# Filler products and a bias product 64 columns wide, fewer fillers, and no mark of each pair's buffer, in a fused attention and feed-forward kernel

## What is computed

```python
xn = layernorm(x)                                   # without weights
# attention: 16 heads of 64
a = layernorm(xn) * ln_w + ln_b
q, k, v = (einsum('bsd,hde->bshe', a, W) + b for W, b in ((W_q, b_q), (W_k, b_k), (W_v, b_v)))
p = softmax(causal(q k^T * 64 ** -0.5))
attn = einsum('bqhe,hed->bqd', p v, W_o) + b_o
# feed-forward, weights rounded to -1, 0, 1 by their mean magnitude
ffn = relu(xn Wq1^T + b1) Wq2^T + b2
out = x + attn + ffn
```

## Time and profile before

| | us |
|---|---|
| median of 3 runs | 232.82 |
| lowest, highest | 232.67, 234.98 |
| the profiled execution's own time | 233.94 |
| its span, first to last instruction | 232.1 |
| busy: TensorE, its weight loads | 225.7, 191.6 |
| busy: VectorE, ScalarE, GpSimd | 203.8, 195.0, 182.9 |

### The profile page before, as it was taken

How to read it: one execution, slowest core, us unless ns; L and a number is a source line. 1 busy time by engine, 2 the same in 40 slices (tenths; PEclk the granted TensorE clock), 3 DMA queues, 4 the chain that set the end, 5 groups by cost and what they waited for, 6 DMA issues and landing times.

```text
span 232.1 us, 7803 instructions
## 1 busy us (share of the span) xinstructions
PE 225.7 (97%) x2710; PEld 191.6 (83%) x2710; DVE 203.8 (88%) x840; ACT 195.0 (84%) x733; POOL 182.9 (79%) x363
## 2 busy tenths in 40 slices
PE   8999999999999999999999999999989999999995
PEld 8976687888788888888888888888879888778874
DVE  2349995999899999999999899999989999999961
ACT  1279997997799798988899798989899799998840
POOL 6338998899976987899689969899688879888900
PEclk9999997999999999999999999999999999999999
DMA  5970074665347466565557457655656466748810
GB/s 160 314 210 1 6 170 104 138 136 133 89 108 167 102 138 183 135 142 116 118 136 155 103 135 157 140 136 123 140 127 150 80 159 143 152 125 177 204 51 25
DMA packets 24023, 30.67 MB, mean 132 GB/s; under 512 B 2608, under 2 KB 23088, under 8 KB 23984
## 3 DMA queue, kind: packets, MB, share of 16 engines
q1 hardware_dynamic: 23840, 30.16, 55.0%
q10 hardware_dynamic: 144, 0.02, 0.0%
HBM read 4.73 MB, written 1.05 MB: 25 GB/s over the span
## 4 chain that ended last, share of the span: by engine, by line
PE 45%; POOL 21%; DVE 14%; ACT 11%; DMA 4%; issue 2%; SPq 2%; POOLq 0%; DVEq 0%
PE s_ps L818 8%; POOL prob L310 6%; PE m_ps L856 6%; POOL prob L309 5%; DVE s_ps L599 4%; DMA pT<-blocks 4%; PE s_ps L729 4%; ACT prob L486 4%; PE m_ps L783 4%; DVE blocks L612 4%; ACT prob L488 3%; PE m_ps L785 3%; PE m_ps L784 3%; POOL xh_cur L408 3%; POOL xn_cur L389 3%; PE m_ps L860 3%
## 5 line engine op out<-in xcount | busy, mean ns | idle before, releaser
L486 ACT ACTIVATE prob<-s_ps,neg_max 128x256 f32<-128x256 f32 x128 | 68.7, 536 | 12.4 <-DVE neg_max L599 12.3
L310 POOL TENSOR_SCALAR prob<-prob,inv_sum 128x256 f32<-128x256 f32 x126 | 61.3, 486 | 0.0
L309 POOL TENSOR_SCALAR prob<-prob,inv_sum 128x128 f32<-128x128 f32 x126 | 47.8, 379 | 15.7 <-DVE inv_sum L606 15.6
L612 DVE STREAM_TRANSPOSE blocks<-prob 128x768 f32<-128x768 f32 x62 | 58.6, 959 | 1.0 <-POOL prob L310 0.4
L488 ACT ACTIVATE prob<-s_ps,neg_max 128x128 f32<-128x128 f32 x128 | 54.7, 427 | 0.0
L599 DVE CUSTOM_DVE_ANT_0 s_ps<-s_ps,causal 128x256 f32<-128x256 f32 x128 | 54.2, 423 | 0.0
L818 PE MATMUL s_ps<-qk 64*64 64x64 f32 (+2 forms) x1280 | 47.7, 281 | 0.3
L818 PEld LDWEIGHTS s_ps<-qk 64*64 64x64 f32 x1280 | 39.7, 134 | 9.5 <-issue 4.1
L599 DVE CUSTOM_DVE_ANT_0 s_ps<-s_ps,causal_first 128x128 f32<-128x128 f32 x128 | 42.1, 329 | 0.0
L856 PE MATMUL m_ps<-pT,v 128*64 128x256 f32 x256 | 39.9, 389 | 1.5 <-DMA pT<-blocks 1.3
L475 ACT ACTIVATE qk<-m_ps,vecs 128x256 f32<-128x256 f32 x64 | 34.2, 535 | 7.1 <-PE m_ps L779 5.8
(11 more groups left out here) (125 smaller groups left out, 545.2 us busy)
## 6 DMA issues: line engine op xcount, KB each, us to landing
pT<-blocks SPq DMA_DIRECT2D x124, 192.0 KB, 3.6
xT_cur<-in_xT SPq DMA_DIRECT2D x8, 128.0 KB, 2.7
outT<-out_sb SPq DMA_DIRECT2D x8, 128.0 KB, 1.7
x_all<-in_x SPq DMA_DIRECT2D x1, 768.0 KB, 9.0
wv_raw<-in_w_v SPq DMA_DIRECT2D x2, 256.0 KB, 5.2
wo<-in_w_o SPq DMA_DIRECT2D x1, 512.0 KB, 7.0
x_all<-in_x SPq DMA_DIRECT2D x2, 128.0 KB, 4.0
wq_raw<-in_w_q SPq DMA_DIRECT2D x2, 128.0 KB, 2.5
```

What stands on the lines that cost most here:

```text
L309: op(first, first, inv_sum[:, j, 2 + h:3 + h], 0.0, ALU.mult, ALU.add)
L310: last = op(later, later, inv_sum[:, j, h:h + 1], 0.0, ALU.mult, ALU.add)
L486: nc.scalar.activation(later, s_ps[:, pair % 2, h, 0:S].rearrange("p (g j k) -> p g j k", g=TILES, j=QT), ACT.Exp, bias=neg_max[:, j, h:h ...
L612: nc.vector.transpose(blocks[:, duo, :, n, :, :], prob[:, pair % NBUF, :, :, :, :] .rearrange("p h j g k -> p (j g) h k")).then_inc(turned, 1)
```

## The change

Fillers: all of them become 64 columns wide instead of 128, `BUSY` goes from (20, 10) to (20, 6), and the step `wk5:1` goes. `wk3:0` stays. No other step of any list moves; the strings are only broken at other places. The product of V's bias gets a moving operand of 64 columns, all equal, by a broadcast; the bank's first 64 columns are written and column 0 is still what is read. The mark in `maxima` and its buffer go, so the wait for the scores is now ahead of the reduction itself.

```diff
--- before.py
+++ after.py
@@ -45,11 +45,11 @@
 
 
 
-BUSY = (20, 10)
-PE_HEAD = ("xb:0 wk5:1 pr0:0 pr1:3 xn:2 s0 s1 v0:3 pr2:1 pr3:2 v1:3 s2 v2:1 s3 pr4:3 ta:0 pr5:2 pr6:1 s4 pr7:3 "
-           "v3:0 xh+:1 f0:2 s5 wk3:0 s6 pr0+:0 bo:2 f1:1 pr1+:3 s7 xn+:0 z0:1 s0+ pr2+:3 pr3+:2 pr4+:0 s1+ "
-           "pr5+:1 z1:3 s2+ z2:2 s3+ pr6+:0 oa:3 f0+:1 s4+ z3:0 s5+ v0+:1 v1+:2 pr7+:0 ob v2+:1 v3+:2 xh++:3 "
-           "f1+:0 s6+ s7+ z0+:1 pr0++:0 pr1++:2 pr2++:3 xn++:0 pr3++:1 s0++")
+BUSY = (20, 6)
+PE_HEAD = ("xb:0 pr0:0 pr1:3 xn:2 s0 s1 v0:3 pr2:1 pr3:2 v1:3 s2 v2:1 s3 pr4:3 ta:0 pr5:2 pr6:1 s4 pr7:3 v3:0 "
+           "xh+:1 f0:2 s5 wk3:0 s6 pr0+:0 bo:2 f1:1 pr1+:3 s7 xn+:0 z0:1 s0+ pr2+:3 pr3+:2 pr4+:0 s1+ pr5+:1 "
+           "z1:3 s2+ z2:2 s3+ pr6+:0 oa:3 f0+:1 s4+ z3:0 s5+ v0+:1 v1+:2 pr7+:0 ob v2+:1 v3+:2 xh++:3 f1+:0 s6+ "
+           "s7+ z0+:1 pr0++:0 pr1++:2 pr2++:3 xn++:0 pr3++:1 s0++")
 PE_PLAN = ("z1-:2 s1 pr4:3 v0:0 pr5:2 v1:1 pr6:3 s2 s3 oa-:2 f0:3 z2-:1 z3-:0 s4 s5 pr7:1 v2:3 ob- v3:3 xh+:0 "
            "f1:2 s6 s7 z0:0 pr0+:1 pr1+:2 pr2+:3 pr3+:1 xn+:0 s0+")
 PE_TAIL = ("pr4:2 s1 z1-:3 v0:0 s2 pr5:1 pr6:0 s3 z2-:2 s4 pr7:3 s5 z3-:1 oa-:0 f0:3 s6 s7 f1:1 v1:3 v2:2 v3:1 "
@@ -188,7 +188,6 @@
 
         pT = sb("pT", [P, DUOS, QT, 3, 2, 2, QB])
         neg_max = sb("neg_max", [P, NBUF, 4])
-        slot_mark = sb("slot_mark", [P, NBUF])
         row_sum = sb("row_sum", [P, NBUF, 4])
         inv_sum = sb("inv_sum", [P, NBUF, 4])
 
@@ -593,7 +592,6 @@
                     dve.wait_ge(masks, 4)
                 if h == 0:
                     wait(dve, s_psd, PAIRS * b + pair + 1)
-                    nc.vector.tensor_copy(slot_mark[:, j:j + 1], causal[:, 0:1])
                 for col, cols, mask in ((h, slice(0, S), causal[:, :]), (2 + h, slice(S, W), causal_first[:, :])):
                     sc = s_ps[:, pair % 2, h, cols]
                     last = nc.vector.tensor_tensor_reduce(out=sc, in0=sc, in1=mask, scale=-SCALE, scalar=-MASKED,
@@ -726,9 +724,9 @@
             def stay_busy(n, into):
 
                 for _ in range(n):
-                    nc.tensor.matmul(into, ones[:, :], ones[:, :], start=True, stop=True)
-
-            stay_busy(BUSY[0], s_ps[:, 1, 1, 0:P])
+                    nc.tensor.matmul(into, ones[:, :], ones[:, 0:E], start=True, stop=True)
+
+            stay_busy(BUSY[0], s_ps[:, 1, 1, 0:E])
             pe.wait_ge(ident_set, 1)
 
             def wait_taken(step):
@@ -888,7 +886,7 @@
                 pe.wait_ge(wo_in, 16)
                 pe.wait_ge(vec_in, 16)
                 for p in range(PAIRS):
-                    last = nc.tensor.matmul(bank("bo", 0, 0)[:, 0:1], wo[:, p, :], vecs[:, BV + p:BV + p + 1],
+                    last = nc.tensor.matmul(bank("bo", 0, 0)[:, 0:E], wo[:, p, :], vecs[:, BV + p:BV + p + 1].broadcast_to([P, E]),
                                             start=(p == 0), stop=(p == PAIRS - 1))
                 last.then_inc(out_bias_psd, 1)
 
@@ -980,11 +978,11 @@
                     turn_heads_input(b)
                 elif kind == "xb":
                     turn_first_heads_input(kind)
-                    stay_busy(BUSY[1], s_ps[:, 1, 1, 0:P])
+                    stay_busy(BUSY[1], s_ps[:, 1, 1, 0:E])
                 elif kind == "xn":
                     turn_hidden_input(b)
                 elif kind == "wk":
-                    stay_busy(index, bank(kind, index, b)[:, 0:P])
+                    stay_busy(index, bank(kind, index, b)[:, 0:E])
                 else:
                     total_ffn()
```

## The result

The changed kernel takes 235.5 us (median of 13, 234.69 to 236.47); the kernel before, timed beside it, 233.34 (231.57 to 236.04). The ratio is 1.0109, 95% interval 1.0075 to 1.0142: slower by 1.1%. The profiled execution took 235.85 us, with a span of 234.1 and a mean granted clock of 1.0. The forecast was 229.2 us, the range 227.6 to 234.4. The time is outside it, and on the other side of no change.

What follows compares the result with a forecast made beforehand. VectorE and TensorE together were taken to set the middle's pace, with fillers holding the start. 233.94 less 2.0 (start), 1.0 (bias product) and 1.7 (marks) gave 229.2 us, range 227.6 to 234.4.

Steps and rivals of the forecast that it cites:

- the clock rises as before: Start: 64-column fillers in an unbroken row raise TensorE's clock as 128-column ones did, between 6 and 7 us.
- the sum: Whole kernel: 233.94 less 2.0 (start), 1.0 (bias product) and 1.7 (marks) gives 229.2 us.
- The late clock: Rival at the start: fillers run low, first projection at 12.5, 2.2 us later less 1.7 for marks, 233.3 us; chance 0.37.
- upper bound of 236.0: Upper end of the late-clock rival: marks 0.7, fall at the bias product still there, low stretch up to twice as long.
- The pace of narrow products: Fillers: weight load sets the pace, so 64 columns save 0 to 7 ns a record at high level; 213 ns at low.
- The rival of shorter products: Rival at the start: narrow fillers take 107 ns at low level, projections start 4.7 us earlier, 228.1 us; chance 0.05.
- The fillers' count: Start: 18 fewer filler records at 0.112 us bring the first projection 2.0 us earlier, all of it counting.
- x2T is ready 0.7 us before the fillers end: Start: the first projection's input is ready at 9.29, fillers end at 9.97, so the fillers still last longest.
- V's bias product: Bias product at 64 columns: same 1.7 us; if it keeps the clock up, gain 0 to 1.7, taken as 1.0.
- runs near 232.8 don't have it: Kernel before: runs near the 232.82 median lack the clock's fall at 33.9, since its 1.0 is about the difference.
- The marks: Removing 64 one-column copies on VectorE, 60 ns each in place, gains 1.7 us.
- the bounds 0.7 and 3.8: Marks' gain: lower from 12 of 64 on the chain of work, upper from all 64 at 0.06 us.

Runs made afterwards that it cites:

- e4: Kernel before with all fillers 64 columns wide, counts as before: 240.29 us, ratio 1.0297.
- e1: Changed kernel with all fillers back at 128 columns, counts (20, 6) kept: 230.58 us, ratio 0.988 to before.
- e11: e10 with 9 fewer fillers, (20, 6) and wk5 out, all 128 columns wide, marks in: 231.04 us.
- e10: Kernel before with V's bias product alone 64 columns wide, same kernel as e3 on another chip: 232.43 us, ratio 0.9945.
- e12: e1 with fillers cut to BUSY (20, 2): 229.68 us, ratio 0.9835.
- e3: Kernel before with V's bias product alone 64 columns wide: 232.51 us, ratio 0.9953.
- e8: Same kernel as e1, run again on another chip: 230.15 us.
- e7: e1 with V's bias product back at one column: 230.67 us.
- e2: Kernel before without the marks and their buffer, nothing else changed: 232.33 us, ratio 0.9929.

## Why the prediction was wrong, step by step

**The step that failed** is "I take it, narrowly, that the clock rises as before". Products of 64 columns in an unbroken row did not raise it, in 12 us of the changed kernel and in 15 of e4, and the same number at 128 columns did: the first 40 records took 6.1 to 7.6 us in the traces with wide fillers and 8.79 in both with narrow ones. That step alone is worth 4.9 us (e1 against the changed kernel), which is more than the whole gain that the sum had. With the clock risen, which is e1, the rest of the change gave 230.6 us where the sum had 229.2.

**The rival named it.** The late clock had a chance of 0.37, a time of 233.3 and the reason that the clock fell behind one-column products although weight loads ran through them, so weight loads don't keep it up. By the rows that reason was better than mine for the forecast, which was that the row of products had no gap and that 64 columns are far from one. The terms: first projection at 12.5, measured 12.5 on the timeline (12.71 in the chain); low stretch behind it 3.4 us, measured 4.1, to the rise at 16.6, in which the projections, two transposes and nothing more ran. The start lost 2.8 us where the rival had 2.2, the marks gave 1.1 at most where it had 1.7, and the kernel before stood at 233.3 and not 232.8; some 0.5 of the 2.2 us between its 233.3 and the measured 235.5 stays open. The range ended at 234.4, inside this rival's own upper bound of 236.0; it should have gone there, since the bound had been worked out. (That bound adds 1.7 us once, though it names two things, the fall at the bias product and a longer low stretch.)

**The pace of narrow products** held: 105 to 112 ns at the high level, 204 to 220 at the low one. The rival of shorter products falls. (Its fillers would have ended at 1.04 + 4.3 = 5.3 us, not 5.5; nothing hangs on it.) The Trainium skill's "TensorE: Matmul & The Clock Gate" gives a weight load, in "LDWEIGHTS (loading the stationary operand)", the time of its columns over 1.2 per ns, so 107 ns for 128 by estimate; the moving width does not stand in it. The 105 to 112 ns at the high level agree, the 204 to 220 at the low one do not. Its smaller figure for 1 to 64 columns, in "Back-to-back issue gap", is one for a product by itself; the same section says that in a stream of loads and products both set the spacing, and the prediction read the figure as if it were for such a stream.

**The fillers' count**: 18 x 0.112 = 2.0 us held for the first projection (e11). 1.4 of it was measured in the medians (e10, e11). That x2T is ready 0.7 us before the fillers end held too: with four records in place of twelve TensorE waits 0.32 us for it (e12).

**V's bias product**: same time at 64 columns, right (1.73 against 1.68). That it keeps the clock up where one column lets it fall, right for the kernel before (e3, e10). The size: behind the stretch the fall had cost 1.5 us, within the bound of 1.7, and 0.7 to 0.8 was left at the last scores where 1.0 was taken. That runs near 232.8 don't have it fits the two groups, but that over half of all executions do was not seen; in the median the width brings 0.5% (e3, e10), about 1.2 us.

**The marks**: at the lower end of the bounds 0.7 and 3.8, at 0.7 to 1.1 and not 1.7. That end, counted from the chain of work, was the better guide; VectorE's small idle time in the middle was not, for its waits for scores grew instead, 3.2 to 5.3 us.

**The sum from the parts**, in medians: +4.9 (narrow fillers), -1.4 (fewer), -1.1 (marks), -1.2 (bias product) = +1.2 us. Measured +2.2. The parts come from three chips and from medians over executions with and without the fall, and the difference stays unassigned. One trace points at the marks: the changed kernel's 199.0 us from the first scores to the last is no shorter than the 199.0 and 199.1 of e3 and e10, which have the marks. But the two traces of one kernel, e1 and e8, differ by 1.2 us there (198.9, 197.7), so this does not show it.

## What to carry to other kernels

Work that only keeps TensorE's clock up has to be judged by whether the granted clock, or the records' durations, changed after it. A product made narrower saves no time where its weight load sets the pace, and can lose the one thing that it was for. When one kernel's executions fall into two groups, look at the mean granted clock of each before comparing medians: here they lay 1% apart, and about half of the executions were in each. Then look in the traces where the difference arises; not all of it came from the place where the clock fell. And where two cases hang on one unknown of the clock, the range has to reach the far end of both.

## What the runs showed of the hardware

- Products of 64 columns with a 128 x 128 stationary operand of f32 left the clock at its low level for as long as they ran (up to 15 us, e4); with 128 columns it rose, by the fillers' durations, between about 4 and 7 us on the traces' scale, differing from execution to execution.
- The same width, 64 columns, was enough not to lose the high level in the bias product, where with one column the mean clock shows a fall in 34 of 62 executions. There it stood for 1.7 us between dense products, which is not the fillers' case; no run here tells whether it would also hold the level for longer.
- One column didn't lose it in any of 12 executions when the start was 2 us shorter (e7), but did in 4 of 12 with the start as before (e2) and in 2 of 5 with it 4.6 us longer (e4). Whether the place in time decides, and why, stays open.
- The stretch at the low level, 3.4 us long, cost 1.5 us behind it and 0.7 to 0.8 us at the last scores (before against e3 and e10).
- At the low level weight load and product together keep half the pace: 204 to 220 ns a record whether 64 or 128 columns follow, 105 to 112 at the high level with 1 to 128.
- A copy of one column on VectorE, 0.14 us long and 60 ns in place, cost 0.7 to 1.1 us over 64 of them, and the second and third 1.5 us each.
